# GpSimd's indirect DMAs wait for TensorE's expansion signal as well, in three passes of a four-layer graph network

## The reference

```python
x = _layernorm(x + _L0_gnn_ref(x, edge_index, edge_type_4, ...))    # relation attention, 4 edge types
x = _layernorm(x + _L1_gnn_ref(x, edge_index, edge_attr_64, ...))   # messages: two-layer MLP per edge
x = _layernorm(x + _L2_gnn_ref(x, ..., node_type_3, src, dst))      # 8-head attention, node types
x = _layernorm(x + _L3_gnn_ref(x, edge_weight, src, dst))           # weighted sum over the edges
```

## Time and profile before

| what | us |
|---|---|
| median of three runs | 3320.36 |
| span of the profiled execution, first to last instruction | 3278.8 |
| time around the span (the median less the span) | 41.6 |
| TensorE busy | 2119.1 |
| GpSimd busy | 1686.9 |
| VectorE busy | 1616.3 |
| ScalarE busy | 1177.9 |

### The profile page before, as it was taken

How to read it: one execution, slowest core, us unless ns; L and a number is a source line. 1 busy time by engine, 2 the same in 40 slices (tenths; PEclk the granted TensorE clock), 3 DMA queues, 4 the chain that set the end, 5 groups by cost and what they waited for, 6 DMA issues and landing times. The chain is left out here.

```text
span 3278.8 us, 39377 instructions
## 1 busy us (share of the span) xinstructions
PE 2119.1 (65%) x9903; PEld 1708.7 (52%) x9903; DVE 1616.3 (49%) x4408; ACT 1177.9 (36%) x3337; POOL 1686.9 (51%) x1704
## 2 busy tenths in 40 slices
PE   5335676879783778888772175766577755555467
PEld 2225565757662667667651165655555433333367
DVE  3236777776841234423331144566577754444356
ACT  2245555555421223333221144444445322222234
POOL 3466655565104556666615545656545666666600
PEclk9655555555556889899885555555557775666579
DMA  6544434343103223232214333334332222222255
GB/s 233 204 132 125 121 102 118 108 126 106 44 9 86 65 66 83 67 82 69 80 36 118 89 102 108 110 112 118 107 88 65 74 69 69 68 74 68 67 190 173
DMA packets 244607, 322.35 MB, mean 98 GB/s; under 512 B 105346, under 2 KB 160931, under 8 KB 243045
## 3 DMA queue, kind: packets, MB, share of 16 engines
q0 software_dynamic: 66560, 163.90, 17.5%
q1 hardware_dynamic: 177797, 155.67, 15.6%
HBM read 257.60 MB, written 63.38 MB: 98 GB/s over the span
## 5 line engine op out<-in xcount | busy, mean ns | idle before, releaser
L1318 POOL DMA_INDIRECT e_gathered<-msg_src_table,src_idx x416 | 398.9, 959 | 422.0 <-POOLq L364 165.6
L692 POOL DMA_INDIRECT e_gathered<-rel_src_table,rel_idx x416 | 431.1, 1036 | 344.4 <-ACT e_gathered L891 145.2
L1866 POOL DMA_INDIRECT e_kv<-kv_table,src_idx x416 | 406.0, 976 | 368.9 <-DVE e_weighted L2236 164.1
L1879 POOL DMA_INDIRECT rows_by_src<-e_kv,e_row x416 | 425.4, 1022 | 260.4 <-DVE e_kv L2165 131.0
L1953 PE MATMUL e_ps_q<-e_window,e_spread 64*128 64x128 f32 x1664 | 350.7, 380 | 218.7 <-issue 125.2
L1953 PEld LDWEIGHTS e_ps_q<-e_window,e_spread 64*128 64x128 f32 x1664 | 308.0, 277 | 293.2 <-issue 281.7
L2088 ACT ACTIVATE e_spread<-e_offsets,e_minus_lane 64x512 f32<-64x512 f32 x208 | 149.1, 717 | 673.0 <-remote 389.6
L750 PE MATMUL e_ps_r<-e_window,e_spread 64*128 64x128 f32 x832 | 211.2, 429 | 178.8 <-DMA e_window<-rel_dst_table 104.4
L750 PEld LDWEIGHTS e_ps_r<-e_window,e_spread 64*128 64x128 f32 x832 | 181.7, 319 | 207.8 <-DMA e_window<-rel_dst_table 135.0
L1988 PE MATMUL e_ps_a<-e_onehot,e_weighted 128*128 128x66 f32 x832 | 190.5, 401 | 146.9 <-DVE e_weighted L2236 88.0
L1988 PEld LDWEIGHTS e_ps_a<-e_onehot,e_weighted 128*128 128x128 f32 x832 | 171.5, 304 | 170.6 <-DVE e_weighted L2236 121.2
(11 more groups left out here) (445 smaller groups left out, 4301.4 us busy)
## 6 DMA issues: line engine op xcount, KB each, us to landing
n_rows<-rows_by_src SPq DMA_DIRECT2D x26, 1032.0 KB
e_offsets<-group_offsets SPq DMA_DIRECT2D x208, 128.0 KB
e_keys<-tile_keys SPq DMA_DIRECT2D x104, 128.0 KB
e_window<-rel_dst_table SPq DMA_DIRECT2D x416, 32.0 KB
e_mixed<-in_edge_attr_dram SPq DMA_DIRECT2D x103, 128.0 KB
rel_src_table<-t_up SPq DMA_DIRECT2D x5, 2560.0 KB
e_gathered<-rel_src_table,rel_idx POOLq DMA_INDIRECT x416
e_gathered<-msg_src_table,src_idx POOLq DMA_INDIRECT x416
```

Source lines behind the costliest of these rows:

```text
L692: pool.indirect_dma_start(gathered[:, q % GS, j, :], None, rel_table, bass.IndirectOffsetOnAxis(ap=rel_idx[:, q * J + j:q * J + j + 1], ax ...
L1318: pool.indirect_dma_start(gathered[:, q % GS, j, :], None, msg_table, bass.IndirectOffsetOnAxis(ap=src_idx[:, q * J + j:q * J + j + 1], ax ...
L1866: pool.indirect_dma_start(kv[:, q % RING, j, :], None, kv_table, bass.IndirectOffsetOnAxis(ap=src_idx[:, q * J + j:q * J + j + 1], axis=0) ...
L1879: pool.indirect_dma_start(in_order, bass.IndirectOffsetOnAxis(ap=row[:, q // 2 % RS, q % 2 * J + j:q % 2 * J + j + 1], axis=0), kv[:, slot ...
```

## The change

One wait is added in each of three places, ahead of the four indirect DMAs of a group. In the relation pass GpSimd also waits until `expanded` has reached q, which is when groups 0 to q - 1 are expanded. In the head pass it waits for q - 4, which is when groups 0 to q - 5 are expanded (no wait for the first five). In the scatter it waits until the expansion of the next row group is done.

```diff
@@ rel_layer, pool_program
                 for q in range(Q):
                     hold(pool, reduced, q - GS + 1)
+                    hold(pool, expanded, q)
                     pool.nop(nofuse=True)
@@ head_and_rows, pool_program
                 for q in range(Q):
                     hold(pool, weighed, q - RING + 1)
+                    hold(pool, expanded, q - 4)
                     pool.nop(nofuse=True)
@@ head_and_rows, send_rows
                     pool.wait_ge(taken, number[True, q] + 1)
+                    pool.wait_ge(expanded, number[True, min(q + 1, Q - 1)] + 1)
                     pool.wait_ge(tagged, q + 1)
```

## The result

The changed kernel takes 3151.57 us (median of four runs, 3141.19 to 3160.26), the kernel before 3320.18 us (four runs, 3301.15 to 3322.48). The ratio is 0.9516 (95% interval 0.9484 to 0.9548), 4.8% faster.

A forecast was written before the change was run, and what follows sets the result against it. The prediction took no engine as full, but signals between other engines as delayed during GpSimd's long unbroken runs of indirect DMAs. Its terms, -25 - 5 - 12 + 0 - 3 = -45 us, gave 3275 us from 3320.36, own range 3245 to 3310, wider range 3195 to 3340.

The forecast's parts named there:

- a signal between other engines: Kernel before, during long unbroken runs of indirect DMAs: such a signal seems to take up to 19 us to arrive.
- Head pass, start: First 24 head groups: the gather run breaks at about 50 us instead of 120; -25 us, bounds -7 to -75.
- if the first 24 ran at the later pace: Head pass start: at 6.62 us a group, group 23 would be joined 161 us after the start, a gain of 39.
- Head pass, rest: Later 80 head groups: delayed gathers are hidden and runs break sooner; -5 us, bounds +10 and -30.
- Relation pass, start: First relation groups, issued in one run before: join 2 at about 137 instead of 149.37; -12 us.
- Relation pass, rest: Later relation groups: +8 us for late gathers, -8 for shorter runs; bounds +60 and -96.
- Rival 1: Relation pass: the tight wait becomes its loop, 10.6 us a group; slower, 3345 us; chance 0.16.
- Scatter: Scatter: second group of each four starts 1.6 us later, partly regained; -3 us, bounds +42 and -30.
- Can return as much: Scatter: the added gap falls into a 20 us run that slows the others, so it may regain its cost.
- The base: Whole kernel: span 3278.8 us plus 41.6 around it stands for the median 3320.36.
- rival 3: All gathers settle into the messages pass's rhythm, 6.32 us a group: relation gains 96, head 37; 3187 us; chance 0.22, whole or half.
- Rival 2: Whole kernel: no change, 3320 us, since each group uses up a shared resource equally whenever its DMAs go; chance 0.12 (with a fourth).

The follow-up runs named there:

- e12: Signal test alone (TensorE and VectorE to and fro beside GpSimd's DMAs), third chip: rounds up to 5.6 us instead of 1.18 beside 48 unbroken indirect DMAs.
- e10: Kernel before plus GpSimd waiting for its own last landing ahead of every second group, relation and head passes, third chip: 3184.05 us, ratio 0.9608.
- e9: The changed kernel with all three waits, run again on the third chip against the kernel before: 3154.67 us, ratio 0.9505.
- e8: Signal test alone (TensorE and VectorE to and fro beside GpSimd's DMAs), on the chip without delay: 1.18 us a round in every section.
- e4: Kernel before plus GpSimd waits on VectorE instead of TensorE in relation and head passes, none new in the scatter: 3248.41 us, ratio 0.9913.
- e1: Kernel before plus only the relation pass's added wait: 3232.61 us, ratio 0.9863.
- e7: Kernel before plus tighter waits (expanded q + 1 in relation, q - 1 in head, none in scatter), chip without delay: 2789.17 us, ratio 1.0233.
- e3: Kernel before plus only the scatter's added wait: 3252.11 us, ratio 0.9932.
- f1: Changed kernel plus landing waits ahead of every second scatter group, fourth chip, ratio against the kernel before: 3185.31 us, 0.9701.
- f3: Changed kernel plus landing waits every second group in relation and scatter, every third in head, fourth chip, against the kernel before: 3195.83 us, ratio 0.9711.
- g1: The changed kernel once more on the third chip, against the kernel before at 3310.47 us: 3147.52 us, ratio 0.9507.
- e11: Kernel before plus looser waits (expanded q - 2 in relation, q - 8 in head, none in scatter), third chip: 3247.77 us, ratio 0.9811.
- e2: Kernel before plus only the head pass's added wait: 3213.27 us, ratio 0.980.
- f4: Signal test alone, fourth chip, indirect DMAs in runs of 48, 16, 12 and 8: up to 5.6, up to 4.2, 1.18 and 1.18 us a round.
- f2: Kernel before plus landing waits only, every second group in relation and scatter, every third in head, fourth chip: 3195.75 us, ratio 0.9725.
- e5: Kernel before plus GpSimd waiting for its own last landing ahead of every second relation and head group, chip without delay: 2895.44 us, ratio 1.0628.
- e6: Kernel before plus looser waits (expanded q - 2 in relation, q - 8 in head, none in scatter), chip without delay: 2724.51 us, ratio 0.9995.

## Why the prediction was wrong in size

*The mechanism was right*, as far as it went. Long unbroken runs of GpSimd's indirect DMAs make signals late, and the waits break them: e12 shows the delay with no other work in the program, e10 gets the whole gain of e9 in the relation and head passes from breaks alone (1507.7 us for both against 1512.2), and on the chip where e8 shows no delay the same breaks cost 6.3%. The part that I had as "a signal between other engines" is narrower: in the rows above it is TensorE's signal to VectorE, not the way back. It is also longer: the pairing of the expansion at 1785.60 with join 3 was off by one group, and joins 3 and 4 are 39 and 41 us behind their own expansions. e4 limits the account: its relation pass lost 63 us of lateness and became no shorter.

*Head pass, start*: forecast -25, measured -38.2 (join 23 at 162.2 us after the first gather instead of 200.4), in its bounds of -7 to -75. The reckoning "if the first 24 ran at the later pace", 161 us, hit the place; I then took a third off for the lost quiet time, and nothing was lost.

*Head pass, rest*: forecast -5, measured -38.4 (from join 23 to join 103 it took 529.6 us and now takes 491.2). This is the step that failed, outside its bound of -30: the price of shorter runs over the whole pass. It was taken as -5 here, -8 in the relation pass's rest and -3 in the scatter, 16 us together; these three parts measured -38.4, -20.6 (with the loss that stood against it) and -21.3, 80 us. Its words were that "the delay of the gather is hidden" and that "a run breaks sooner", which is so. But I priced a broken run at nearly nothing, though the earlier trace rows had a price: 29% busy on VectorE in a run against 64% behind it. The time of runs beyond their first 10 us falls from 261 to 176 us in the head pass, and the lateness from 204 to 117. By those shares, as an estimate, 85 us fewer of such time are worth 85 x (1 - 29 / 64) = 46 us, still short of the 74.8 of the whole head pass but far from 5. The join comes 35 to 54 us behind the gather after group 23, somewhat more than the 35 to 45 that I read.

*Relation pass, start*: forecast -12; join 2 is 16.0 us earlier, join 22 17.9 (24.5 in e1). Right within its size.

*Relation pass, rest*: forecast +8 - 8 = 0, measured -20.6 from join 22 to join 103 (578.0 to 557.4; -22.0 in e1). The loss was there, 36 us of lateness of gathered rows in 18 or 19 joins; the gain, taken as 8, was about 90 us less lateness of signals. Rival 1 had the right place and too small an opponent. e7, with both waits one and three groups tighter, loses 2.3% where there is no delay to save, all of it in the relation pass. The waits that bind there number 103, not 104, since the first group's is for a count of zero.

*Scatter*: forecast -3, measured -21.3 (-26.3 in e3), within its bound of -30. "Can return as much" was too little: lateness fell by 37 us.

*Messages pass*: whether +15.9 in these two executions has to do with the change is not settled. The pass takes 729.7 to 743.5 us in e1 to e4 and 735 to 745 in f1 to f3. On the third chip it takes 755.7 and 757.6 with the change (e9, g1), 748.6 in e10 and 742.0 in e11, so part of it goes with the chip and up to some 10 us may go with the change.

*The base*: I put 41.6 us around the span. It was 2.1, and the profiled execution was 39 us quicker than the median. For the forecast it made no difference, since the sum was a difference.

*The rivals*: rival 3 had the head pass (653 / 104 = 6.28 us a group against the messages' 6.32 in the earlier trace rows) and not the relation pass, which stays at 715, over the 690 that I had set for it. I gave it 0.22 "in whole or half", and the range reached only to 3195. Rival 2 is refuted by e2 alone, whose head pass is 84 us shorter. The rule of the Trainium skill ("SBUF — State Buffer", section "SBUF: two separate sides"), by which DMA and compute don't slow each other, does not fit e12, where the rounds share no data with the gathers; but it isn't the bytes that slow them, since 48 DMAs of the same size by SyncE or plain ones by GpSimd leave the round at 1.18 us. For those the trace agrees with the rule, and the rule says nothing of signals.

What stays open: what it is that holds TensorE's updates up. In e12 the delay needs 21 us of unbroken issuing to begin (14 with SyncE's loads) and 7.6 us to end, and it shows on three of four chips, which looks like something that queues. The missing records in e12 and in every kernel trace of those three chips point at the recording as a part of it, and no unrecorded time was taken. So whether the kernel is slow, and the change a gain, when nothing records it is not shown.

## What to carry to other kernels

Where an engine stands idle long after its input is ready, look at what a third engine does at that moment: here 12 indirect DMAs in a row were harmless with nothing beside them (f4), 16 and 48 were not, and in the kernel 8 left less delay than 12 (e10, f2). Price such a delay over the whole pass, by the busy share inside and behind a run, not by its most visible case. A break costs something itself (2.1 to 2.7 us beyond the usual 0.30 between two issues, medians of 2.5 us idle in e10 and 3.0 in f1), so try it pass by pass: it paid in two passes and not in the scatter. And run the old kernel on more than one chip, and once without the profiler: what gained 1.9 and 3.9% on one chip (e11, e10) gave nothing and lost 6.3% on another, and the chips differ in what their traces lose.

## What the hardware showed that I had not expected

- The same kernel takes 2724 us on one chip and 3280 to 3312 on three others, at a like granted clock (0.52 and 0.51 in the head pass). The head pass takes 655 us there in e5 and 539 in e6, where the changed kernel needs 654 here.
- TensorE's signal reaches VectorE up to 4.5 us late in e12 beside an unbroken run of indirect DMAs, and 39 and 41 us after the expansion's end for two groups of the kernel before, while VectorE's reaches TensorE in 0.05 us.
- On the three chips with the delay the trace holds 26 to 34% of the updates by DMAs in the kernel, on the fourth 96 or 97%.
- Behind an indirect DMA that gathers 128 rows GpSimd goes on 2.1 us (f4) to 2.5 us (e10, median) after its end if it waits for the landing; behind one that scatters 128 rows in f1 the landing shows 2.7 us after the end.
- A looser and a tighter wait cost 0% and 2.3% on the chip without delay, and the looser one gains 1.9% with it.
